# Windowed attention of a fused four-layer kernel: keys prepared one slot earlier, ScalarE and VectorE queues reordered, and the last layer norm of a row moved into the MLP

## What is computed

```python
h = shift_token(x)                       # upper 64 channels from the token before
q, k, v = split(h @ wqkv, 3)             # 8 heads of 64
q = l2norm(q) * qs;  k = l2norm(k) * ksc
q, k = rotary_xpos(q, k)
o = local_attention(q, k, v)             # windows of 64, keys of this window and the one before
x = x + o @ wo
h = layernorm(shift_token(x)) * lg + lb
a, g = split(h @ w1 + b1, 2)
x = x + (a * gelu(g)) @ w2 + b2
```

## Time and profile before

| | us |
|---|---|
| median of 3 runs | 1405.4 |
| the runs | 1404.46, 1405.4, 1411.82 |
| the profiled execution, device time | 1395.94 |
| its span | 1394.1 |
| busy PE / DVE / ACT / POOL | 1195.4 / 1006.4 / 909.3 / 578.4 |

### The profile page before, as it was taken

One profiled execution on the slowest core, in us unless ns is written; L12 is line 12 of the kernel. 1 busy time (PEld: TensorE's weight loads), 2 busy tenths in 40 slices (PEclk: granted clock), 3 DMA queues, 4 the chain that ended last, 5 costly groups with the idle time before them and its releaser, 6 DMA issues.

```text
span 1394.1 us, 28067 instructions
## 1 busy us (share of the span) xinstructions
PE 1195.4 (86%) x10484; PEld 693.8 (50%) x10484; DVE 1006.4 (72%) x2420; ACT 909.3 (65%) x2161; POOL 578.4 (41%) x554
## 2 busy tenths in 40 slices
PE   7887048759999999999978999997888879898878
PEld 5333048724555555555434666653555534555543
DVE  3455842248889889899664999995788954788864
ACT  4664002227777777777777888874888853788862
POOL 1022037624444444444230222224778731778740
PEclk9997559968999999999999999998999999999999
DMA  9002107430000000000010000000000000000000
GB/s 331 4 0 61 58 15 239 137 110 0 1 2 1 1 1 0 1 1 1 29 78 1 2 2 2 2 2 33 2 2 2 2 1 0 2 1 2 2 2 30
DMA packets 20677, 40.68 MB, mean 29 GB/s; under 512 B 3859, under 2 KB 13595, under 8 KB 19902
## 3 DMA queue, kind: packets, MB, share of 16 engines
q1 hardware_dynamic: 18494, 37.14, 7.9%
q0 software_dynamic: 2048, 1.74, 0.5%
HBM read 33.17 MB, written 6.55 MB: 28 GB/s over the span
## 4 chain that ended last, share of the span: by engine, by line
PE 74%; DVE 9%; issue 6%; ACT 5%; POOL 4%; DMA 1%; SPq 0%; POOLq 0%; DVEq 0%; ACTq 0%
PE bank L1111 5%; PE bank L1124 5%; PE bank L1503 5%; PE bank L1491 5%; PE pair L1082 5%; PE bank L1481 4%; PE bank L1509 4%; PE bank L1098 3%; PE pair L1098 3%; PE bank L2260 3%; PE pair L1085 2%; PE pair L1740 2%; PE pair L1995 2%; PE bank L1975 2%; PE bank L1131 2%
## 5 line engine op out<-in xcount | busy, mean ns | idle before, releaser
L1332 POOL TENSOR_TENSOR rope_part<-rope_part,rope_tab 128x512 f32<-128x512 f32 x64 | 81.4, 1272 | 195.1 <-DVE rope_part L1251 195.0
L1183 ACT ACTIVATE soft<-bank,neg_max 128x512 f32<-128x512 f32 (+2 forms) x192 | 100.5, 536 | 27.9 <-DVE neg_max L1259 27.7
L2198 POOL TENSOR_TENSOR win_part<-win_part,scaled_tab 128x512 f32<-128x512 f32 x64 | 81.7, 1277 | 81.0 <-DVE win_part L2134 80.6
L1556 POOL TENSOR_TENSOR win_soft_alibi<-win_soft_alibi,win_inv_alibi 128x384 f32<-128x384 f32 x64 | 51.6, 826 | 147.9 <-DVE win_inv_alibi L1540 147.8
L1195 ACT ACTIVATE softT<-bank 128x512 f32<-128x512 f32 x160 | 92.5, 599 | 30.7 <-PE bank L1111 30.6
L1098 PE MATMUL bank<-k_rope,q_rope 64*128 64x512 f32 (+3 forms) x384 | 97.3, 479 | 1.6 <-POOL k_rope L1337 1.6
L1259 DVE CUSTOM_DVE_ANT_0 bank<-bank,att_mask 128x512 f32<-128x512 f32 (+2 forms) x192 | 92.2, 522 | 6.9 <-PE bank L1098 6.9
L1516 ACT ACTIVATE win_soft_local<-bank,win_neg_max_local,rq 128x128 f32<-128x128 f32 x256 | 92.7, 477 | 0.0
L1111 PE MATMUL bank<-ident,soft 128*128 128x128 f32 x640 | 89.5, 279 | 0.6 <-ACT softT L1195 0.5
L277 POOL TENSOR_SCALAR h<-ln_norm,mod 128x512 f32<-128x512 f32 x28 | 24.3, 866 | 155.7 <-DVE ln_norm L261 155.7
L1275 DVE TENSOR_SCALAR soft<-soft,exp_inv 128x128 f32<-128x128 f32 (+2 forms) x160 | 87.5, 594 | 1.1
(11 more groups left out here) (406 smaller groups left out, 3383.0 us busy)
## 6 DMA issues: line engine op xcount, KB each, us to landing
moe_w<-in_moe_w SPq DMA_DIRECT2D x8, 960.0 KB, 5.4
y_tok<-in_moe_w SPq DMA_DIRECT2D x8, 960.0 KB, 5.1
y_dram<-zeros SPq DMA_DIRECT2D x8, 256.0 KB
htok_dram<-htok SPq DMA_DIRECT2D x2, 1024.0 KB
y_tok<-y_dram SPq DMA_DIRECT2D x8, 256.0 KB, 4.8
att_w<-in_att_w SPq DMA_DIRECT2D x1, 1536.0 KB, 7.6
att_w<-in_local_w SPq DMA_DIRECT2D x1, 1536.0 KB, 9.6
wmod<-in_wmod SPq DMA_DIRECT2D x1, 1152.0 KB, 7.4
```

The lines of the kernel that those rows point to most:

```text
L1183: nc.scalar.activation(soft[par][:, hd, TILE_AT[t]:TILE_AT[t] + keys(t)], score_bank(u, s, hd)[:, at:at + keys(t)], ACT.Exp, scale=-1.0, b ...
L1332: nc.gpsimd.tensor_tensor(rope_part[2 * piece + 1][:, :], rope_part[2 * piece + 1][:, :], rope_tab[:, 2 * piece + 1, :], ALU.mult).then_in ...
L1556: nc.gpsimd.tensor_tensor(a["soft"][u % 2][:, js, :], a["soft"][u % 2][:, js, :], a["inv"][:, u % 2, js].unsqueeze(2).to_broadcast([128, 4 ...
L2198: nc.gpsimd.tensor_tensor(swapped, swapped, scaled_tab[:, 2 * j + 1, :], ALU.mult) \
```

## The change

Key work (projection, square, sum, logarithm, exp, rotation, `key`) moves from unit s+2 to unit s+3 in slot s; semaphore targets of the interleaved steps come from two new helpers, `query_at` and `key_at`. On ACT, `key_log` moves from behind the 8 exps to ahead of them and `key_root` between the two halves. On DVE, `add` moves ahead of the first `sums`, and `key` ahead of the second `sums`. Layer norm of row 3 moves into the MLP: its PE steps to f = 2 and f = 3, its ACT and DVE steps behind step 3. The centring and variance of row 2 move one place earlier. Cut to its core:

```diff
+        def query_at(W, name, u):
+            return W.start[name] + {"win_proj": 3 * u + 2, "win_sum": 4 * u + 4,
+                                    "win_rs": min(2 * u + 3, 2 * W.units)}.get(name, 2 * u + 2)
+        def key_at(W, name, u):
+            return W.start[name] + {"win_proj": max(3 * u, 1), "win_sum": 4 * u + 2,
+                                    "win_rs": max(2 * u, 1)}.get(name, 2 * u + 1)
...
@@ local_pe @@
-                if piece == 0 and p == 0:
+                if piece == 1 and p == 0:
                     pe.wait_ge(sem("shifted"), 8 * l + b + 1)
+                if piece == 1 and u >= 2:
+                    pe.wait_ge(sem("win_v_read"), W.at("win_v_read", u, -1))
...
-                if piece == 2:
-                    pe.wait_ge(sem("win_turned"), W.at("win_turned", u, 2))
+                if piece == 2 and u + 1 < W.units:
+                    pe.wait_ge(sem("win_turned"), key_at(W, "win_turned", u + 1))
...
-                on(W, project, s + 2, 1)
+                on(W, project, s + 3, 1)
                 on(W, query_sums, s + 2)
                 on(W, transpose, s, 1)
-                on(W, key_sums, s + 2)
+                on(W, key_sums, s + 3)
...
                 if left == 1:
                     ln_variance(pe, k, 1)
+                    ln_centred(pe, k, 2)
...
                 if left == 1:
-                    ln_centred(pe, k, 2)
-            ln_variance(pe, k, 2)
+                    ln_variance(pe, k, 2)
@@ local_act @@
-                on(W, square, s + 2, 1)
+                on(W, square, s + 3, 1)
                 on(W, query_log, s + 2)
                 on(W, transposed, s, 1)
...
+                on(W, key_log, s + 3)
                 on(W, exps, s + 1, 0)
+                on(W, key_root, s + 3)
                 on(W, exps, s + 1, 1)
-                on(W, key_log, s + 2)
-                on(W, key_root, s + 2)
...
             ln_root(act, k, 2)
-            ln_squared(act, k, 3)
-            ln_root(act, k, 3)
@@ local_dve @@
-                on(W, rotate, s + 2, 1)
+                on(W, rotate, s + 3, 1)
                 if 2 <= left < 5:
                     shift_dve(dve, 4 - left)
+                on(W, add, s - 1)
                 on(W, sums, s + 1, 0)
-                on(W, add, s - 1)
                 on(W, inverse, s + 1, 0)
+                on(W, key, s + 3)
                 on(W, sums, s + 1, 1)
                 on(W, inverse, s + 1, 1)
-                on(W, key, s + 2)
+            ln_normed(dve, k, 2)
             dve.wait_ge(sem("pair_added"), W.after()["pair_added"])
             shift_dve(dve, 3)
-            ln_normed(dve, k, 2)
-            ln_normed(dve, k, 3)
@@ mlp_pe @@
             up(0)
-            ln_centred(pe, 8 + l, 3)
-            up(1)
-            ln_variance(pe, 8 + l, 3)
-            down(0)
-            for f in range(1, 3 * B):
+            for f in range(3 * B):
                 if f + 1 < 3 * B:
                     up(f + 1)
+                if f == 2:
+                    ln_centred(pe, 8 + l, 3)
+                if f == 3:
+                    ln_variance(pe, 8 + l, 3)
                 down(f)
@@ mlp_act, behind the Gelu @@
+                if f == 12 * l + 3:
+                    ln_squared(act, 8 + l, 3)
+                    ln_root(act, 8 + l, 3)
@@ mlp_dve, behind the product @@
+                    if f == 12 * l + 3:
+                        ln_normed(dve, 8 + l, 3)
```

More of the change, by code:

```diff
@@ L1956, in project @@
                 w = att_w[:, LP * l + p, piece, :]
-                if piece == 0 and p == 0:
+                if piece == 1 and p == 0:
                     pe.wait_ge(sem("shifted"), 8 * l + b + 1)
+                if piece == 1 and u >= 2:
+                    pe.wait_ge(sem("win_v_read"), W.at("win_v_read", u, -1))
+                elif piece == 1 and u:
+                    pe.wait_ge(sem("win_turned"), key_at(W, "win_turned", 0))
+                elif piece == 1:
+                    pe.wait_ge(sem("ln_normed"), 32 + 4 * l)
                 if piece == 0 and u:
-                    pe.wait_ge(sem("win_log"), W.at("win_log", u, -1))
+                    pe.wait_ge(sem("win_log"), query_at(W, "win_log", u - 1))
                 elif piece == 0 and l:
                     pe.wait_ge(sem("mlp_added"), 3)
-                elif piece == 0:
-                    pe.wait_ge(sem("ln_normed"), 31)
-                if piece == 1 and u:
+                if piece == 2 and u + 1 < W.units:
+                    pe.wait_ge(sem("win_turned"), key_at(W, "win_turned", u + 1))
+                elif piece == 2:
                     pe.wait_ge(sem("win_v_read"), W.at("win_v_read", u))
-                elif piece == 1:
-                    pe.wait_ge(sem("ln_normed"), 32 + 4 * l)
-                if piece == 2:
-                    pe.wait_ge(sem("win_turned"), W.at("win_turned", u, 2))
                 if piece < 2:
@@ L1979, in query_sums @@
             def query_sums(u):
[L1980 to L1983, removed]
+                pe.wait_ge(sem("win_sq"), query_at(W, "win_sq", u))
+                pe.wait_ge(sem("win_turned"), query_at(W, "win_turned", u))
+                pe.wait_ge(sem("win_log"), key_at(W, "win_log", u))
                 for k in range(4):
@@ L1992, in key_sums @@
             def key_sums(u):
-                pe.wait_ge(sem("win_sq"), W.at("win_sq", u, 2))
-                pe.wait_ge(sem("win_log"), W.at("win_log", u, 1))
+                pe.wait_ge(sem("win_sq"), key_at(W, "win_sq", u))
+                if u:
+                    pe.wait_ge(sem("win_log"), query_at(W, "win_log", u - 1))
                 pe.matmul(bank[1][:, :], head_sum[:, :], a["sq"][:, 1, :], start=True, stop=True) \
@@ L2084, in take_values @@
             def take_values(u):
-                act.wait_ge(sem("win_proj"), W.at("win_proj", u, 3))
+                act.wait_ge(sem("win_proj"), W.start["win_proj"] + min(3 * u + 4, 3 * W.units))
                 if u >= 3:
@@ L2129, in rotate @@
             def rotate(u, j):
-                dve.wait_ge(sem("win_sq"), W.at("win_sq", u, j + 1))
+                place = key_at if j else query_at
+                dve.wait_ge(sem("win_sq"), place(W, "win_sq", u))
                 if u:
-                    dve.wait_ge(sem("win_sum"), W.at("win_sum", u, 2 * j - 2))
+                    dve.wait_ge(sem("win_sum"), place(W, "win_sum", u - 1))
+                if u and j:
+                    dve.wait_ge(sem("win_k"), W.at("win_k", u))
                 nc.vector.tensor_tensor(win_part[2 * j][:, :], bank[5 * j][:, :], scaled_tab[:, 2 * j, :], ALU.mult)
@@ L2148, in key @@
             def key(u):
-                dve.wait_ge(sem("win_sum"), W.at("win_sum", u, 4))
-                dve.wait_ge(sem("win_rs"), W.at("win_rs", u, 1))
+                dve.wait_ge(sem("win_sum"), key_at(W, "win_sum", u))
+                dve.wait_ge(sem("win_rs"), key_at(W, "win_rs", u))
                 if u >= 2:
@@ L2196, in rotate @@
                 swapped = win_part[2 * j + 1][:, :]
-                pool.wait_ge(sem("win_turned"), W.at("win_turned", u, j + 1))
+                place = key_at if j else query_at
+                pool.wait_ge(sem("win_turned"), place(W, "win_turned", u))
                 nc.gpsimd.tensor_tensor(swapped, swapped, scaled_tab[:, 2 * j + 1, :], ALU.mult) \
                   .then_inc(sem("win_sum"), 1)
-                pool.wait_ge(sem("win_sum"), W.at("win_sum", u, 2 * j + 1))
+                pool.wait_ge(sem("win_sum"), place(W, "win_sum", u) - 1)
                 if j == 0 and u >= 2:
```

19 lines of the change are left out of this document (10 added, 9 removed).

## The result

The changed kernel takes **1422.9 us** (median of 7 runs, 1419.33 to 1425.34), the kernel before 1411.8 beside it (7 runs, 1404.46 to 1414.72). The ratio is 1.0095, 95% interval 1.0069 to 1.0120: slower by 0.95%, about 13.4 us, where 9.4 were forecast.

What follows compares the result with a forecast made beforehand. A loop, not one engine, bounds the steady slot: scores, maxima, exps, key's logarithm and exp, `key`, then POOL's loop after the change. 15.7 - 1.2 - 1.2 - 3.9 = +9.4 on 1405.4 gives 1414.8 us; own range 1409 to 1421.

Steps and rivals of the forecast that it cites:

- The steady slot: Local layers: a loop through POOL and DVE makes each slot 10.47 instead of 9.755, +15.7 us over 22 slots.
- from reciprocal to reciprocal (1077.47 to 1078.39) is one `sums` and one `inverse`: Steady slot on DVE: second `sums` and `inverse`, now between `key` and the query rotation, cost 0.92.
- That the other edits cost nothing in a steady slot: Steady slot: `key_log` ahead of the exps, `add` ahead of `sums` and PE's new waits cost zero.
- POOL does not bind: Rival, steady slot: the loop over `key_log` sets the slot at 9.35, total 1390.2 us; chance 0.06.
- The front of a layer: Layer start: first scores 0.7 later in layer 0, 2.4 in layer 1; with the two slots behind, -1.2 together.
- The two slots behind the front: First two slots after a layer's first scores: 19.2 instead of 21.47, without the wait on their own key.
- The last two slots: Layer end: no key work left in the last slot with projections, second slot falls by 0.6, -1.2 both layers.
- The MLP: MLP of both layers: earlier first `down` gains 14.3, row 3's norm and three table loads return 10.4, net -3.9.
- 0.5 for a clock that drops again: MLP, behind the stall at row 3's root: a lower PE clock costs 0.5 per layer.
- `key` does not win the port: Rival, steady slot: `key` goes before POOL's division, slot 9.64, total 1396.6 us; chance 0.13.
- the meetings are not half but whole: Rival, steady slot: `key` held but scaled maxima free, slot 9.83, total 1400.8 us; chance 0.15.
- The clock falls: Rival, steady slots: PE's clock drops with more idle, slots reach 11.0, total 1426.5 us; chance 0.06.

Runs made afterwards that it cites:

- 5: Changed kernel with `key` last in DVE's slot and ACT's `key_log` and `key_root` back behind the 8 exps; 1389.8 us.
- experiment 6: Changed kernel with `key` last in DVE's slot and `add` back behind the first `sums`; 1395.8 us, ratio 0.9995.
- experiment 1: Changed kernel with `key` moved back behind the second `sums` and `inverse` on DVE; 1392.9 us, ratio 0.9987.
- experiment 10: Changed kernel with only each layer's first key product, `key(0)`, moved behind the first query's rotation on DVE; 1403.6 us.
- experiment 11: Changed kernel with `key` last, `key(0)` behind the first query's rotation, and the joint Ln and Exp table set requested before row 3's root; 1385.4 us, ratio 0.9935.
- experiment 8: Kernel before with only the MLP part of the change and row 2's earlier centring and variance; 1390.6 us, ratio 0.9975.
- experiment 3: Changed kernel with `key` back behind the second `sums` and `inverse`, and POOL's first division waiting for `key`; 1435.3 us.
- experiment 4: Kernel before with one DVE line moved: `key` ahead of the second `sums` and `inverse`, keys still at unit s+2; 1414.9 us.
- experiment 2: Changed kernel with one added wait: POOL's first division of a slot waits for `key`; 1396.2 us, ratio 1.0007.

## Why the prediction was right and wrong

**The steady slot** was right in its mechanism and 0.12 too long. `key` is ended by POOL's addition, not by ACT, and lasts 1.51, the figure of the other meeting in the earlier trace rows. The 1.52 from division to `sums` measured 1.51, the 1.28 for the scaled maxima 1.27. The Trainium skill ("SBUF — State Buffer", SBUF: two separate sides) has whichever of the two engines starts first keep the shared port pair for the whole instruction. The trace agrees on who waits, while by the 1.04 of the division's record the loop would be 10.5 and it is 10.36. The term that is too large is "from reciprocal to reciprocal (1077.47 to 1078.39) is one `sums` and one `inverse`", 0.92. From `sums` to its reciprocal is 0.71 (1060.69 to 1061.40), so 0.2 of it was a gap that I carried over; the rotation follows the reciprocal after 0.09: 0.80. That is 2.6 us over 22 slots. The other 2.0 are the first steady slots of each layer, 9.43 and 10.27, which were counted as full ones. Together +11.1 for +15.7.

**That the other edits cost nothing in a steady slot** held: 5 and 6 leave it at 9.56. "POOL does not bind" gave 9.35 if ACT's loop were the slot; experiment 1 has the nearest thing, 9.56, and it needs exactly the order that the change gave up. Keys one slot ahead make 9.755 into 9.56 when `key` stays last: in the slot the earlier keys pay, their place in DVE's queue does not.

**The front of a layer is the step that failed**: "first scores 0.7 later in layer 0 and 2.4 later in layer 1 ... Together −1.2". They came 3.5 and 4.0 later, together with the slots behind them +4.7. The prediction gives no working for 0.7 and 2.4. It names `key(0)` ahead of the query's rotation, but has no term for the time in which that rotation stands ready behind `key(0)`, nor one for the query's projection. DVE in layer 1:

```profile
1203.69 0.69 DVE L2167 SCALAR_TENSOR_TENSOR win_k<-win_rs_local,win_part 128x512 f32<-128x512 f32 x1 [2.73 <-POOL win_part L2218]
1204.30 0.68 DVE L2147 TENSOR_TENSOR win_part<-pair,scaled_tab 128x512 f32<-128x512 f32 x1
```

and PE beside it:

```profile
1205.73 0.64 PE L1999 MATMUL pair<-head_sum,win_sq_local 64*64 64x1 f32 x32 [3.44 <-issue]
1206.84 2.04 PE L2007 MATMUL pair<-win_sq_local,head_sum 128*128 128x512 f32 x2 [0.47 <-ACT log_q L2075]
```

`key(0)` waits 2.73 for POOL, and the query's rotation stands behind it though its data lie ready from 1202.54, when ACT's square ends. PE is then idle 3.44 and comes back at the lower level (2.04 for what takes 1.10 in experiment 10). Experiment 10 moves this one `key` and has 1.8 of the 4.0 back; the 2.2 that stay are close to the forecast 2.4. So in layer 1 the missing term is this wait.

In layer 0 the wait behind `key(0)` is the smaller part: the query's square ends at 980.56 and its rotation starts at 981.32. The larger part is PE's order. In the kernel before, the query's projection goes out first, 1.05 behind the variance, while the layer norm is still under way:

```profile
957.34 1.10 PE L1972 MATMUL pair<-shifted,att_w 128*128 128x512 f32 x2
```

In the changed kernel it stands behind the key's projection, which waits for the layer norm, and behind the key's sums, and goes out 7.55 behind the variance, at a granted 0.50:

```profile
978.01 1.91 PE L1984 MATMUL pair<-shifted,att_w 128*128 128x512 f32 x2
```

With that the query's sums start 12.29 behind the variance instead of 7.59, and from there to the scores it is 5.55 for 6.74: +3.5. This is read from the two traces; no run puts the query's projection back in front. Of the 2.4 that experiment 10 has back here, most is the clock (experiment 11 has the same edit and 0.5 back).

The two slots behind the front were put at 19.2. Layer 1 has 19.13 at a granted 1.00, layer 0 has 20.54 at 0.92.

**The last two slots** gave −2.5 for −1.2: `add` ahead of `sums` works there as well (1.2 per layer in experiment 6), which I had at zero. It is paid back in part in the next stretch, +0.7 per layer, where DVE's layer norm sits.

**The MLP** gave −0.45 with the stretch ahead of it, for −3.9. The +1.4 of that stretch belongs to `add`: it takes 14.74 in experiment 6, with `add` late, and 14.74 in experiment 8, which has the MLP's edit alone. So the MLP's own part is −1.8. The three loads around row 3, the bound that I took, are there:

```profile
1169.20 1.28 ACT L238 ACT_TABLE_LOAD   x1
1172.02 0.69 ACT L238 ACTIVATE ln_log<-pair,eps_col 128x512 f32<-128x512 f32 x1 [1.54 <-PE pair L207]
1172.73 1.28 ACT L243 ACT_TABLE_LOAD   x1
1174.02 0.63 ACT L243 ACTIVATE ln_rstd<-ln_log 128x512 f32<-128x512 f32 x1
1174.67 1.28 ACT L2306 ACT_TABLE_LOAD   x1
1175.96 1.26 ACT L2306 ACTIVATE mlp_gelu<-bank,vec 128x512 f32<-128x512 f32 x2
```

The stall is 3.24 for 2.9:

```profile
1177.80 1.12 PE L2285 MATMUL bank<-win_part,w 128*128 128x512 f32 x2 [3.24 <-DVE win_part L2328]
```

and the first `down` starts 5.4 behind the first `up` instead of 10.6, 5.2 sooner for the 4.5 of layer 0; in layer 1 it is 6.0 for 5.5. What I had put too low is the price of the clock behind the stall, "0.5 for a clock that drops again": 1.7 in this trace (16.88 for 15.19) and nothing in others. A small term was missing as well: DVE's update of h and the shift stood between row 3's norm and the fifth product, which started at 1176.99, some 0.4 later than its Gelu allowed (1175.96 and half of the 1.26 that two take). In timed runs this part is worth more than its trace shows: taking it out raised the ratio from 1.0095 to 1.0162 (different groups of runs; their intervals overlap by 0.0005), and alone it gave −2.7 and −2.5. So −3.9 lies between the −1.8 of one trace and the −5.2 of another, and the means of experiment 8's paragraph give −2.9: the one trace of the changed kernel shows 1.1 less than they do.

**The sum** came out near by luck: a steady term too large by 4.6 and last slots better by 1.3 stood against fronts (with the slots behind them) worse by 5.9 and an MLP with the stretch ahead of it worse by 3.4: 9.4 − 4.6 − 1.3 + 5.9 + 3.4 = 12.8. Of the 8.1 between the forecast time (1414.8) and the measured one (1422.9), 6.4 is the kernel before itself, 1411.8 beside the change for the 1405.4 that the forecast started from.

**The rivals**: `key` does not win the port, and the meetings are not half but whole. The clock falls in single slots only in experiment 3; the changed kernel's steady stretch is at 1.00 throughout.

## What to carry to other kernels

Before moving an instruction forward in an engine's queue, ask what it will wait for there and what of ready work stands behind it; an operand that comes from a slower engine belongs behind the work that is ready. Where one engine releases an instruction of another and goes straight on with its own next one, look whether the two meet: in the steady slots here POOL went first by 0.08 each time, and a wait added to it made the loop shorter. Look at the first slots and the ends of a pipelined loop on their own: a `key` ahead of ready work cost 0.8 in each steady slot and 1.8 once in layer 1's front, and in layer 0's front, by its two traces, work that waits now stands ahead of work that had filled the wait.

## What the runs showed of the hardware

A division on POOL that is recorded at 1.04 held DVE's `key` for 0.82 (1.51 for 0.69, started 0.08 behind it), not for its whole length. In every trace a `key` that started less than 0.90 behind a division ended 1.58 to 1.61 behind the division's start: 0.08 and 1.51 in the changed kernel, 0.37 and 1.22 in experiment 4, 0.48 and 1.11 in the kernel before, 0.77 and 0.82 in experiment 1. At 0.89 to 0.90 behind it took its own 0.69. POOL's queue started its next instruction 0.07 to 0.08 ahead of the DVE instruction that POOL itself had released, in the steady slots of the changed kernel. And around stalls of about 3 us in the MLP the same code had a granted clock of 1.00 in some executions and of 0.83 to 0.95 in others, worth up to 3 us in layer 0 (42.18 in experiment 1, 39.18 in experiment 2).
